# A DLRM tower: ten tables looked up by one-hot matmuls where it was twelve, and the Gram of two samples in one matmul

## The chip, the cores and the metric

The kernel runs on one core of a Trainium2 chip. The time is that of one launch on the device, in microseconds (us), from the first to the last instruction with what the launch itself takes around them. The engines are TensorE (PE in the profile; PEld is its weight load), VectorE (DVE), ScalarE (ACT), GpSimd (POOL) and SyncE (SP, whose queue SPq issues transfers). They run on their own and wait for each other by semaphores.

## The reference

512 samples; each has a dense vector of 128 and one row out of each of 26 tables (one of 125,000 rows, nine of 12,500, eight of 1,250, eight of 1,000; rows of 128). The products of all pairs of its 27 vectors go with the dense vector through three layers.

```python
e = jnp.stack([tbl_0[ids[:, 0]], ..., tbl_25[ids[:, 25]]], axis=1)
combined = jnp.concatenate([dense_features[:, None, :], sparse_features], axis=1)
interactions = jnp.einsum('bnd,bmd->bnm', combined, combined)
interactions_flat = interactions[:, _TRIU_I, _TRIU_J]
z = jnp.concatenate([dense_features, interactions_flat], axis=1)
h = jnp.concatenate([z, r_dense_features], axis=1)
h = jnp.maximum(h @ W_top1 + b_top1, 0.0)
h = jnp.maximum(h @ W_top2 + b_top2, 0.0)
y = h @ W_top3
```

All is float32.

## The kernel before

The samples are taken in four tiles of 128. `vecs_t` (128 x tile x pair of samples x slot x 2) holds, for each sample, its vectors as columns: slot 0 the dense vector, then the tables, and five slots repeated, so that 32 columns of a sample stand side by side. Two ways fill it.

Fourteen tables are **gathered**: GpSimd issues one indirect DMA for each table and tile (`gather`, L316), 56 in all, group by group; a group is up to four slots, a tile four groups, so there are 16 groups. PE transposes a group (`turn`, L401) into one of two PSUM tiles `turned`, and VectorE or ScalarE copies it to `vecs_t` (`copy_slots`, L257; `VECTOR_TURNS` says which are VectorE's). Group n is gathered when `turn` n - 3 is done (`AHEAD` = 2).

Twelve small tables are **looked up** for all 512 samples at once, as products with one-hot matrices. SyncE loads a table whole (`load_table`, L248, three buffers; a load waits until the table three before it is split). ScalarE rounds it to fp32r (`table_hi`, L556), VectorE takes the rest (`table_lo`, L496). A table has 8 or 10 blocks of 125 rows; per block a one-hot matrix of 125 x 512 is made, 6 or 8 of them by VectorE (`make_one_hot`, L488, up to four blocks a comparison) and two by ScalarE (L581, L589). PE multiplies all blocks with `table_hi` (L416), then with `table_lo` (L421), and ScalarE copies the sums to `vecs_t` (L565). The ids that are compared must stand on all partitions: those of table 0 are spread by two matmuls with ones (L450), those of the others by three broadcast DMAs into `ids_all` (L285). The one-hot ring has 16 blocks, the sums have four PSUM buffers.

Then, tile by tile, `products` (L437) computes the Gram of each sample: 128 matmuls of 32 columns by 27, each with its own weights, in turn on four column groups of PE's array, into one of two PSUM buffers `gram`. VectorE and ScalarE copy what is wanted of it to `prods` in 20 copies each (`copy_products`, L268). `layer1` (L350 to L355), `layer2` (L371) and `layer3` (L386) follow; ScalarE applies bias and ReLU, VectorE copies y.

The order on each engine is written by hand: `LOOK_TURNS` (each look-up and the turns behind it), then `TENSOR_STEPS`, `VECTOR_STEPS` and `SCALAR_STEPS`. On PE: the look-ups with turns 0 to 13, products 0, turn 14, products 1, turn 15, products 2 and 3 with layer 1 of tiles 0 and 1 in pieces between them, and the rest of the layers. SyncE issues the weights after table 6.

## Time and profile before

| | |
|---|---|
| median of 3 runs | 135.03 us (133.61 to 135.52) |
| the profiled execution's own time | 133.31 us |
| its span | 131.5 us |
| mean granted clock of TensorE | 0.948 |
| PE busy | 107.2 us (82%), 1534 matmuls |
| PE weight loads | 87.1 us (66%), 1534 |
| VectorE busy | 84.2 us (64%) |
| ScalarE busy | 83.7 us (64%) |
| GpSimd busy | 60.5 us (46%) |
| moved by DMA | 15.87 MB |

A row of a timeline gives the start, the length, the engine and line, the operation with output and inputs, the count, and in brackets how long the engine was idle before and what ended that. A float32 matmul stands in the trace as two passes, each a weight load and a matmul, so the 512 Gram matmuls are 1024 in it; an fp32r matmul or a transpose is one pass. Times of one matmul overlap with the next; the distance from start to start is what a stream of them costs. "issue" is idle time for which the profile shows no releaser. The granted clock is 1.00 at 2.4 GHz and 0.50 at 1.2 GHz.

### The profile page before, as it was taken

The numbers are of one execution on the slowest core, as the hardware profiler recorded it, in microseconds if no ns is written. First come the engines' busy times: TensorE is split into PE (matmuls) and PEld (weight loads), VectorE is DVE, ScalarE is ACT, GpSimd is POOL, SyncE is SP. The second block draws the span as 40 slices with busy tenths as digits, with TensorE's granted clock in tenths as the row PEclk, the third lists the DMA queues.
The fourth block names the chain that finished last, engine by engine and source line by source line (L and its number), as shares of the span: only waits on it lengthen the run. The fifth ranks groups of instructions, "written<-read, shape, count | busy, mean of one in ns | idle before, by whom it ended". The sixth has DMA issues, their size and how long they took to land.

```text
span 131.5 us, 3642 instructions
## 1 busy us (share of the span) xinstructions
PE 107.2 (82%) x1534; PEld 87.1 (66%) x1534; DVE 84.2 (64%) x133; ACT 83.7 (64%) x193; POOL 60.5 (46%) x64
## 2 busy tenths in 40 slices
PE   0139998899993199999989994857799779999993
PEld 0117877555862188888857583656698779997981
DVE  1089999599999457999999900794923923920000
ACT  4389394599999854999977050754813943973112
POOL 2687878878878667788697885000000000000000
PEclk9999999999999869999999999555999999999999
DMA  4999999999999979274111122000000000000000
GB/s 98 220 299 287 363 368 253 253 221 260 388 278 232 212 151 250 60 188 109 45 40 40 40 60 59 11 5 5 5 5 0 7 5 5 0 0 5 0 0 1
DMA packets 4812, 15.87 MB, mean 121 GB/s; under 512 B 1630, under 2 KB 1630, under 8 KB 4540
## 3 DMA queue, kind: packets, MB, share of 16 engines
q1 hardware_dynamic: 2850, 11.45, 32.1%
q0 software_dynamic: 1792, 3.67, 11.7%
q10 hardware_dynamic: 154, 0.51, 1.2%
q8 instruction: 12, 0.20, 0.7%
q14 instruction: 4, 0.03, 0.1%
HBM read 15.63 MB, written 0.00 MB: 119 GB/s over the span
## 4 chain that ended last, share of the span: by engine, by line
PE 52%; POOL 19%; issue 12%; DMA 9%; DVE 5%; ACT 0%; DVEq 0%; ACTq 0%
POOL vecs L316 19%; PE gram L437 10%; PE h_ps L352 10%; PE gram L421 9%; PE gram L416 7%; DMA vecs<-tbl,idx 7%; PE turned L371 5%; PE turned L401 4%; PE h_ps L350 3%; DVE one_hot L488 3%; DMA idx<-idx_rows 2%; DVE table_lo L496 2%; PE gram L386 2%; PE h_ps L355 1%; DVE vecs_t L257 1%
## 5 line engine op out<-in xcount | busy, mean ns | idle before, releaser
L316 POOL DMA_INDIRECT vecs<-tbl,idx x56 | 59.7, 1065 | 20.0 <-issue 15.8
L488 DVE TENSOR_TENSOR one_hot<-ids_all,h_ps 125x2048 fp32r<-125x2048 int32 (+1 forms) x24 | 41.9, 1793 | 1.9 <-PE gram L421 1.9
L416 PE MATMUL gram<-one_hot,table_hi 125*128 125x512 f32 x104 | 31.9, 441 | 3.5 <-DVE one_hot L488 2.2
L268 DVE COPY prods<-gram 32x128 f32<-32x128 f32 (+5 forms) x80 | 19.1, 254 | 20.0 <-PE gram L437 9.2
L416 PEld LDWEIGHTS gram<-one_hot,table_hi 125*128 125x128 f32 x104 | 20.2, 207 | 11.2 <-ACT one_hot L589 3.0
L421 PE MATMUL gram<-one_hot,table_lo 125*128 125x512 f32 x104 | 26.5, 399 | 0.5 <-DVE table_lo L496 0.5
L421 PEld LDWEIGHTS gram<-one_hot,table_lo 125*128 125x128 f32 x104 | 19.9, 193 | 5.7 <-DVE table_lo L496 1.4
L268 ACT COPY prods<-gram 32x128 f32<-32x128 f32 (+5 forms) x80 | 17.4, 235 | 8.5 <-PE gram L437 7.0
L437 PE MATMUL gram<-vecs_t 128*32 128x27 f32 x1024 | 14.3, 208 | 6.7 <-issue 6.5
L437 PEld LDWEIGHTS gram<-vecs_t 128*32 128x32 f32 x1024 | 12.3, 126 | 9.2 <-issue 8.5
L496 DVE TENSOR_TENSOR table_lo<-table,table_hi 125x1024 fp32r<-125x1024 f32 (+1 forms) x12 | 15.7, 1308 | 1.9 <-ACT table_hi L556 1.9
L589 ACT ACTIVATE one_hot<-distance,one 125x512 fp32r<-125x512 f32 x24 | 15.9, 711 | 1.6 <-PE gram L421 1.5
L565 ACT COPY vecs_t<-gram 128x512 f32<-128x512 f32 (+1 forms) x12 | 9.7, 807 | 10.6 <-PE gram L421 10.6
L352 PE MATMUL h_ps<-prods,w_sb 128*128 128x128 f32 x112 | 15.9, 279 | 0.0
L556 ACT CAST table_hi<-table 125x1024 fp32r<-125x1024 f32 (+1 forms) x12 | 13.4, 1115 | 3.5 <-DMA table<-tbl 3.5
L581 ACT ACTIVATE distance<-ids_all,row_of 125x512 f32<-125x512 int32 x22 | 14.7, 716 | 0.0
L401 PE MATMUL turned<-ident,vecs 128*128 128x128 f32 x56 | 10.1, 306 | 5.3 <-DMA vecs<-tbl,idx 5.2
L352 PEld LDWEIGHTS h_ps<-prods,w_sb 128*128 128x128 f32 x112 | 13.9, 192 | 0.1
L539 ACT ACTIVATE h<-h_ps,small_sb 128x128 f32<-128x128 f32 x16 | 4.9, 368 | 12.8 <-PE h_ps L355 12.8
L401 PEld LDWEIGHTS turned<-ident,vecs 128*128 128x128 f32 x56 | 7.3, 155 | 7.6 <-DMA vecs<-tbl,idx 6.4
L471 DVE COPY distance<-gram 1x128 f32<-1x128 f32 x4 | 1.1, 279 | 13.0 <-PE gram L386 13.0
L371 PE MATMUL turned<-h,w_sb 128*128 128x128 f32 x64 | 8.1, 280 | 0.0
(33 smaller groups left out, 54.3 us busy)
## 6 DMA issues: line engine op xcount, KB each, us to landing
table<-tbl SPq DMA_DIRECT2D x7, 448.0 KB
table<-tbl SPq DMA_DIRECT2D x4, 560.0 KB
ids_all<-ids_look SPq DMA_DIRECT2D x1, 2048.0 KB, 16.1
w_sb<-w SPq DMA_DIRECT2D x1, 1536.0 KB, 9.5
vecs<-tbl,idx POOLq DMA_INDIRECT x56, 7.0
ids_all<-ids_look SPq DMA_DIRECT2D x1, 512.0 KB, 9.3
w_sb<-w SPq DMA_DIRECT2D x1, 512.0 KB, 10.0
table<-tbl ACTq DMA_DIRECT2D x1, 448.0 KB
```

The source lines that it names most:

```text
L268: return copy(dst.rearrange("p c (h b) -> p c h b", h=HALVES), src.rearrange("p h c b -> p c h b"))
L316: nc.gpsimd.indirect_dma_start(out=vecs[:, t % KEEP, s - 1, :], out_offset=None, in_=tables[f], in_offset=bass.IndirectOffsetOnAxis(ap=idx ...
L352: nc.tensor.matmul(to, w1_sb[:, 1 + c, cols], prods[:, t % 2, c - 1, :], start=False, stop=(c == CHUNKS))
L371: mm = nc.tensor.matmul(h2_ps[o], w2_sb[:, c, o * P:(o + 1) * P], h1[:, t % 2, c, :], start=(c == 0), stop=(c == H1 // P - 1))
L401: mm = nc.tensor.transpose(turned[n % 2][:, i, :], vecs[:, t % KEEP, s - 1, :] if s else dense_rows[:, t, :], ident[:])
L416: nc.tensor.matmul(looked_up[j % SUMS], table_hi[0:TP, j % PARTS, c, :], one_hot[0:TP, k % HOT, :], start=(c == 0), stop=False)
L421: nc.tensor.matmul(looked_up[j % SUMS], table_lo[0:TP, j % PARTS, c, :], one_hot[0:TP, k % HOT, :], start=False, stop=(c == NBLK[j] - 1)). ...
L437: mm = nc.tensor.matmul(gram_cols[t % 2][QUAD * q:QUAD * q + ROWS, blk // HALF, :, blk % HALF], x[:, 0:ROWS], x[:, 0:N], start=True, stop= ...
L488: nc.vector.tensor_tensor(one_hot[0:TP, k % HOT:k % HOT + n, :], ids.to_broadcast([TP, n, B]), rows.to_broadcast([TP, n, B]), ALU.is_equal ...
L496: nc.vector.tensor_tensor(table_lo[0:TP, j % PARTS, 0:NBLK[j], :], table[0:TP, j % RAW, 0:NBLK[j], :], table_hi[0:TP, j % PARTS, 0:NBLK[j] ...
L581: nc.scalar.activation(distance[0:TP, i, :], ids, ACT.Square, bias=at, scale=-1.0).then_inc(distance_ok, 1)
L589: nc.scalar.activation(one_hot[0:TP, k % HOT, :], distance[0:TP, i, :], ACT.Relu, bias=one[0:TP], scale=-1.0).then_inc(hot_act, 1)
```

## The change

- Ten tables are looked up and sixteen gathered (64 gathers). The gathered slots are 1 to 9 and 15 to 21, so a group is always four gathered slots; the third of each tile (slots 9, 15, 16, 17) is copied in two pieces. The slots repeated are now 10 to 14. The dense vectors of all tiles are transposed in one step after look-up 0 and copied by ScalarE.
- The ids of the ten tables are loaded as ten rows. Those of each table are spread by PE, two matmuls of 512 columns with `pick` (ten selector matrices), into four PSUM banks in turn. The broadcast loads are gone.
- `products` takes two samples of one parity in a matmul: 64 columns of weights, 54 moving columns, 64 matmuls a tile, on two column groups. Of the four 32 x 27 blocks of one such product two are used. It fills four PSUM banks, the same for each tile, so it waits for the copies of the tile before. The sums have two buffers in place of four.
- The last look-up is made in two halves of 256 samples. Tile 0's product stands between them. Turns 8 to 15 and layer 1 stand between the later products. VectorE copies turns 1, 3, 5 and all from 7 on.
- The weights are issued after the last table. `AHEAD` is 3.

```diff
-LOOKED_UP = 12
+LOOKED_UP = 10
-SUMS = 4
+SUMS = 2
-AHEAD = 2
-IDS_PARTS = [(1, 2), (2, 4), (4, LOOKED_UP)]
-WEIGHTS_AFTER = 6
+AHEAD = 3
+WEIGHTS_AFTER = LAST
-TURN_AFTER = [0, 1, 2, 3, 4, 5, 5, 6, 7, 8, 9, 10, 11, 11]
+TURN_AFTER = [1, 2, 3, 4, 5, 6, 7, 8]
...
-        gram = [psum(f"gram{i}", [P, HALVES, 512]) for i in range(2)]
+        bank = psum("bank", [P, 2 * BANKS, 512])
+        gram_cols = bank[:, BANKS:, 0:2 * N * RUN].rearrange("p k (m b) -> p k m b", b=RUN)
+        looked_up = [bank[:, j % SUMS, :] for j in range(LAST)]
+        looked_up_half = [bank[:, (LAST + h) % SUMS, 0:B // 2] for h in range(2)]
+        ids_for_dve = [bank[:, BANKS + i, :] for i in range(2)]
+        ids_for_act = [bank[:, BANKS + 2 + i, :] for i in range(2)]
...
+            def spread_ids(j):
+                if j == 0:
+                    pe.wait_ge(pick_ok, 1)
+                    pe.wait_ge(row_f_ok, 1)
+                if j >= 2:
+                    pe.wait_ge(hot_dve, sum(BY_VECTOR[:j - 1]))
+                    pe.wait_ge(distance_ok, BY_SCALAR * (j - 1))
+                for ids in (ids_for_dve[j % 2], ids_for_act[j % 2]):
+                    nc.tensor.matmul(ids, pick[:, j, :], ids_rows_f[:], start=True, stop=True).then_inc(ids_ps_ok, 1)
...
             def look_up(j):
...
+                if j + 2 < LOOKED_UP:
+                    spread_ids(j + 2)
                 pe.wait_ge(lo_ok, j + 1)
...
-            def products(t, layer1_of=None):
+            def products(t):
                 tile_is_out(pe, t)
-                if t == 0:
-                    pe.wait_ge(look_out, LOOKED_UP)
-                if t >= 2:
-                    pe.wait_ge(prods_dve, BY_ENGINE * (t - 1))
-                    pe.wait_ge(prods_act, BY_ENGINE * (t - 1))
-                for blk in range(BLOCKS):
-                    for q in range(QUADS):
-                        r = QUAD * q + blk
-                        x = vecs_t[:, t, r // 2, :, r % 2]
-                        mm = nc.tensor.matmul(
-                            gram_cols[t % 2][QUAD * q:QUAD * q + ROWS, blk // HALF, :, blk % HALF],
-                            x[:, 0:ROWS], x[:, 0:N], start=True, stop=True)
+                pe.wait_ge(look_out, LOOKED_UP + t // 2)
+                if t >= 1:
+                    pe.wait_ge(prods_dve, BY_ENGINE * t)
+                    pe.wait_ge(prods_act, BY_ENGINE * t)
+                for b in range(BLOCKS):
+                    for g in range(P // WIDE):
+                        first = BLOCKS * g + b // 2 * 2
+                        both = vecs_t[:, t, first:first + 2, :, b % 2]
+                        mm = nc.tensor.matmul(gram_cols[WIDE * g:WIDE * (g + 1), b // RUN, :, b % RUN],
+                                              both.rearrange("p x s -> p (x s)"), both[:, :, 0:N],
+                                              start=True, stop=True)
```

On PE, from the end of the look-ups on (L401 a turn, L437 the Gram, L350 and L352 layer 1), before:

```order
L401 MATMUL turned<-ident,vecs 128x128 x7
L437 MATMUL gram<-vecs_t 32x27 x128
L401 MATMUL turned<-ident,vecs 128x128 x4
L437 MATMUL gram<-vecs_t 32x27 x128
L401 MATMUL turned<-ident,vecs 128x128 x3
L437 MATMUL gram<-vecs_t 32x27 x43
L350 MATMUL h_ps<-dense_t,w_sb 128x128
L352 MATMUL h_ps<-prods,w_sb 128x128 x4
L350 MATMUL h_ps<-dense_t,w_sb 128x128
```

The same place of the change (L436 a turn, L484 and L490 a half of the last look-up, L506 the Gram, L371 and L373 layer 1; all PSUM is `bank`):

```order
L436 MATMUL bank<-ident,vecs 128x128 x4
L484 MATMUL bank<-one_hot,table_hi 128x256 x10
L490 MATMUL bank<-one_hot,table_lo 128x256 x10
L436 MATMUL bank<-ident,vecs 128x128 x4
L506 MATMUL bank<-vecs_t 64x54 x64
L484 MATMUL bank<-one_hot,table_hi 128x256 x10
L490 MATMUL bank<-one_hot,table_lo 128x256 x10
L436 MATMUL bank<-ident,vecs 128x128 x8
L506 MATMUL bank<-vecs_t 64x54 x64
L436 MATMUL bank<-ident,vecs 128x128 x4
L371 MATMUL bank<-dense_t,w_sb 128x128
L373 MATMUL bank<-prods,w_sb 128x128 x4
```

The last look-up is in two pieces with product 0 between them, each product has 64 matmuls, and turns and a whole layer 1 stand between products where pieces of layer 1 stood within them.

On VectorE, between the copies of products 0 and 1 (L268 the copies, L257 slots), before:

```order
L268 COPY prods<-gram 21x2x32
L268 COPY prods<-gram 10x2x32
L268 COPY prods<-gram 10x4x32
L257 COPY vecs_t<-turned 128x4x64x2
L268 COPY prods<-gram 32x4x32 x2
L268 COPY prods<-gram 32x2x32 x2
```

The same place of the change (L295 the copies, L282 slots, L579 the sum of the two dense weights):

```order
L295 COPY prods<-bank 10x2x32
L295 COPY prods<-bank 10x4x32
L282 COPY vecs_t<-bank 128x64x2
L282 COPY vecs_t<-bank 128x3x64x2
L282 COPY vecs_t<-bank 128x4x64x2
L579 TENSOR_TENSOR w_sb<-w_sb 128x512
L295 COPY prods<-bank 32x4x32 x2
```

Where one turn's slots stood (turn 14), there are now turns 10 (in two pieces) and 11 and the weight sum.

On SyncE's queue, around the weights (L299 to L301), before:

```order
L248 DMA table<-tbl 13x1024
L299 DMA w_sb<-w 128x3072
L300 DMA w_sb<-w 128x1024
L301 DMA small_sb<-small 128x8
L248 DMA table<-tbl 112x1024
```

The same of the change (L274 the tables, L318 to L320 the weights):

```order
L274 DMA table<-tbl 112x1280
L274 DMA table<-tbl 13x1280
L318 DMA w_sb<-w 128x3072
L319 DMA w_sb<-w 128x1024
L320 DMA small_sb<-small 128x8
L322 DMA y<-distance 1x512
```

The weights have moved behind all tables.

## Rows read from the trace of the kernel before

**Rows 1.** The first line of the page.

```profile
span 131.5 us, 3642 instructions
```

**Rows 2.** The chain of waits: start us, us, what.

```profile
36.50 8.89 DMA vecs<-tbl,idx
...
53.24 1.82 PE gram L421 x8
...
55.06 0.44 PE turned L401 x4
...
57.79 2.27 PE gram L421 x10
...
110.44 1.79 PE turned L371 x16
```

**Rows 3.** Timeline of PE: start us, us, engine, line, operation, count, idle before.

```profile
45.44 1.12 PE L401 MATMUL turned<-ident,vecs 128*128 128x128 f32 x4 [4.89 <-DMA vecs<-tbl,idx]
```

**Rows 4.** Timeline of ScalarE (ACT), same columns, the cast of table 3.

```profile
24.45 1.05 ACT L556 CAST table_hi<-table 125x1024 fp32r<-125x1024 f32 x1 [3.15 <-DMA table<-tbl]
```

**Rows 5.** Timeline of VectorE (DVE): comparisons, and a copy out of a turn.

```profile
7.12 3.42 DVE L488 TENSOR_TENSOR one_hot<-h_ps,row_of 125x2048 fp32r<-125x2048 f32 x2 [5.74 <-PE h_ps L450]
...
11.59 3.41 DVE L488 TENSOR_TENSOR one_hot<-ids_all,h_ps 125x2048 fp32r<-125x2048 int32 x2
...
46.59 0.69 DVE L257 COPY vecs_t<-turned 128x512 f32<-128x512 f32 x1 [2.24 <-PE turned L401]
...
50.29 4.48 DVE L488 TENSOR_TENSOR one_hot<-ids_all,h_ps 125x2048 fp32r<-125x2048 int32 x2 [1.87 <-PE gram L421]
...
56.09 4.55 DVE L488 TENSOR_TENSOR one_hot<-ids_all,h_ps 125x2048 fp32r<-125x2048 int32 x3
```

**Rows 6.** Timeline of PE, Gram matmuls.

```profile
77.72 2.77 PE L437 MATMUL gram<-vecs_t 128*32 128x27 f32 x203
...
82.05 0.76 PE L437 MATMUL gram<-vecs_t 128*32 128x27 f32 x53 [1.55 <-issue]
...
85.72 1.93 PE L437 MATMUL gram<-vecs_t 128*32 128x27 f32 x128 [0.75 <-issue]
...
89.44 1.05 PE L437 MATMUL gram<-vecs_t 128*32 128x27 f32 x58 [1.80 <-issue]
...
97.94 0.93 PE L437 MATMUL gram<-vecs_t 128*32 128x27 f32 x84
...
108.43 0.25 PE L437 MATMUL gram<-vecs_t 128*32 128x27 f32 x3 [0.67 <-issue]
```

**Rows 7.** Windows: stretch, length, busy time (count) by engine, granted clock, DMA.

```profile
82.50:92.60 10.10, 7.32 (x351) 6.22 (x341) 7.36 (x29) 6.26 (x29) 0.00 (x0) 0.50 0.02 5
...
92.80:110.30 17.50, 15.45 (x528) 14.22 (x528) 8.04 (x33) 8.47 (x37) 0.00 (x0) 1.00 0.02 5
```

**Rows 8.** The page: the instruction queue (packets, MB, share), and the gathers' group.

```profile
q8 instruction: 12, 0.20, 0.7%
...
L316 POOL DMA_INDIRECT vecs<-tbl,idx x56 | 59.7, 1065 | 20.0 <-issue 15.8
```

**Rows 9.** DMA issues, all and from 60 to 85 us: count, KB, us to landing.

```profile
ids_all<-ids_look SPq DMA_DIRECT2D x1, 2048.0 KB, 16.1
...
vecs<-tbl,idx POOLq DMA_INDIRECT x15, 2.7
```

**Rows 10.** Timeline of GpSimd (POOL), three of the 56 gathers.

```profile
3.90 1.10 POOL L316 DMA_INDIRECT vecs<-tbl,idx  x1 [2.22 <-DMA idx<-idx_rows]
...
15.29 1.66 POOL L316 DMA_INDIRECT vecs<-tbl,idx  x1 [0.30 <-issue]
...
80.42 0.94 POOL L316 DMA_INDIRECT vecs<-tbl,idx  x1 [0.30 <-issue]
```

**Rows 11.** Timeline of VectorE, the copy of products 0.

```profile
82.85 5.26 DVE L268 COPY prods<-gram 32x128 f32<-32x128 f32 x20 [7.48 <-PE gram L437]
```

**Rows 12.** Timeline of PE, the last matmuls.

```profile
128.95 0.67 PE L386 MATMUL gram<-h,small_sb 128*1 128x128 f32 x4 [0.16 <-ACT h L548]
```

More of the change, by code:

```diff
@@ L47 @@
 GATHERED = by_size[LOOKED_UP:]
-SLOT_TABLE = [None] + GATHERED + LOOKUPS
-TURNED = 1 + len(GATHERED)
+LAST = LOOKED_UP - 1
+GATHERED_SLOTS = list(range(1, FIRST_R)) + list(range(FIRST_V, FIRST_V + len(GATHERED) - FIRST_R + 1))
+LOOKED_UP_SLOTS = [n for n in range(1, N) if n not in GATHERED_SLOTS]
+SLOT_TABLE = [None] * N
+for n, f in list(zip(GATHERED_SLOTS, GATHERED)) + list(zip(LOOKED_UP_SLOTS, LOOKUPS)):
+    SLOT_TABLE[n] = f
 NBLK = [TABLE_ROWS[f] // TP for f in LOOKUPS]
@@ L192, in dlrm_tower @@
         lo_ok = sem("lo_ok")
-        rows_ps_ok = sem("rows_ps_ok")
         one_ok = sem("one_ok")
@@ L222, in looked, with pieces @@
             return FIRST_HOT[j] + NBLK[j]
+        def pieces(n):
+            return len(runs(GROUPS[n % NG]))
         def outs(by_vector, n):
-            return sum(2 if i % NG == 0 else 1 for i in range(n + 1) if (i in VECTOR_TURNS) == by_vector)
+            return sum(pieces(i) for i in range(n + 1) if (i in VECTOR_TURNS) == by_vector)
         def turn_is_out(engine, n):
@@ L362, in mlp2 @@
             def mlp2(t):
+                last = {0: 13, 1: 15}.get(t)
+                if last is not None:
+                    turn_is_out(pe, last - 1)
+                    turn_is_out(pe, last)
                 if t >= 1:
@@ L387, in mlp3, with turn_dense @@
                                           start=(c == 0), stop=(c == H2 // P - 1))
                 mm.then_inc(y_ok, 1)
+            def turn_dense():
+                pe.wait_ge(ident_ok, 1)
+                pe.wait_ge(dense_in, 16)
+                for t in range(TILES):
+                    mm = nc.tensor.transpose(turned[1][:, t, :], dense_rows[:, t, :], ident[:])
+                mm.then_inc(dense_ok, 1)
             def turn(n):
                 t, g = TURNS[n]
-                slots = GROUPS[g]
@@ new lines, in look_up_half @@
+            def look_up_half(h):
+                j = LAST
+                samples = slice(B // 2 * h, B // 2 * (h + 1))
+                pe.wait_ge(look_out, LAST - 1 + h)
+                if h == 0:
+                    pe.wait_ge(hi_ok, j + 1)
+                for c in range(NBLK[j]):
+                    k = FIRST_HOT[j] + c
+                    if h == 0 and c < BY_VECTOR[j]:
+                        pe.wait_ge(hot_dve, sum(BY_VECTOR[:j]) + c + 1)
+                    elif h == 0:
+                        pe.wait_ge(hot_act, BY_SCALAR * j + c - BY_VECTOR[j] + 1)
+                    nc.tensor.matmul(looked_up_half[h], table_hi[0:TP, j % PARTS, c, :],
+                                     one_hot[0:TP, k % HOT, samples], start=(c == 0), stop=False)
+                if h == 0:
+                    pe.wait_ge(lo_ok, j + 1)
+                for c in range(NBLK[j]):
+                    k = FIRST_HOT[j] + c
+                    mm = nc.tensor.matmul(looked_up_half[h], table_lo[0:TP, j % PARTS, c, :],
+                                          one_hot[0:TP, k % HOT, samples], start=False, stop=(c == NBLK[j] - 1))
+                mm.then_inc(half_ok, 1)
@@ L445, in products @@
                 mm.then_inc(gram_ok, 1)
-            pe.wait_ge(ones_ok, 1)
-            pe.wait_ge(row_f_ok, 1)
-            for ids in (ids_for_dve, ids_for_act):
-                nc.tensor.matmul(ids, ones[:], ids_row_f[:], start=True, stop=True).then_inc(ids_ps_ok, 1)
+            spread_ids(0)
+            spread_ids(1)
             for step, i in TENSOR_STEPS:
@@ L453, in _ @@
                     turn(i)
+                elif step == "dense":
+                    turn_dense()
                 elif step == "look":
                     look_up(i)
+                elif step == "look half":
+                    look_up_half(i)
                 elif step == "products":
                     products(i)
-                elif step == "products and layer1":
-                    products(i, i - 2)
                 elif step == "layer1":
@@ L512, in _ @@
                 split_table(j)
-            for n, after in enumerate(TURN_AFTER):
-                if after >= LOOKED_UP - 2 and n in VECTOR_TURNS:
-                    copy_slots(dve, nc.vector.tensor_copy, slots_dve, n)
             for step, i in VECTOR_STEPS:
```

211 lines of the change are left out of this document (107 added, 104 removed).

## The prediction

> **What bounds it now.** I read the page first, then the chain of waits, then each engine's timeline, and last windows of the Gram lines. One profiled execution has a span of 131.5 us [rows 1] and its own time is 133.31 us, so 1.8 us lie outside the span; all sums below are spans of that execution. Its time is 1.3% under the median of 135.03 us.
>
> The span falls into four stretches. (a) Up to about 45 us GpSimd's gathers and the DMA lead: the chain has one gather that takes 8.89 us to land [rows 2], PE stands 4.89 us for it [rows 3], and before that ScalarE stood 3.15 us for table 3 [rows 4]. (b) Up to 77.7 us the look-ups run at VectorE's pace: comparing and splitting one table takes it 4.47 us with 8 blocks (starts 7.12 and 11.59) and 5.80 us with 10 (50.29 and 56.09) [rows 5], while PE needs 2 x 1.82 plus 0.44 us for 8 blocks and a turn, and 2 x 2.27 plus 0.44 for 10 [rows 2]. (c) Up to 108.7 us come the Gram matmuls. In the trace one Gram matmul is two passes of a 32-wide load and 27 columns. 84 passes without a gap take 0.93 us, so (0.93 - 0.19) / 83 = 8.9 ns each, and a tile's 256 would take 2.3 us. They take over 5 (tile 0: 77.72 to 82.81), because PE stands for "issue": [0.75] before 85.72, [1.80] before 89.44, with 128 passes (256 instructions) between them, hence 3.72 us for 256 instructions [rows 6]. From 82.5 to 92.6 us the granted clock is 0.50, the lower level, and PE busy only 7.3 of 10.1 us; after 92.8 it is 1.00 [rows 7]. (d) The rest is MLP work, PE nearly without a gap.
>
> The page names the queue "instruction" with 12 transfers and 0.20 MB [rows 8], which fits refills of about 256 instructions. The Trainium skill (Runtime: NRT & Kernel Launch, Instruction fetch mechanics) says just this: instructions come in blocks of 256. It calls the fetch mostly hidden; the trace disagrees here, with 3.72 us a block in the open.
>
> **The change, part by part.** *Look-ups.* Two 10-block tables go from the look-ups to the gathers. VectorE starts as before, at 7.12 us [rows 5], since the id spread waits for the same kind of small load and cast; `pick` is one copy ahead of that, in idle time. Eight tables x 4.47, two of 5.80, and the slot copies of turns 1, 3, 5 at about 0.6 each [rows 5]: 7.12 + 35.8 + 11.6 + 1.8 = 56.3 us. Reading ids from PSUM costs nothing by the first comparison, which does it already in 3.42 us against 3.41 [rows 5]. The spreads add 2 x 0.227 us to PE per table: 3.64 + 0.44 + 0.45 = 4.5 us, just level with VectorE's 4.47. I cost them at nothing; without this cover they would cost 0.5 x 8 = 4 us. The broadcast id loads disappear (the last moves 2,048 KB and takes 16.1 us to land [rows 9]), and the weights queue behind table 9, whose wait (split of table 6) ends near 39 us; 2 MB then have until 76 us. So the waits of 3.15 and 4.89 us go. After the split at 56.3 PE does 10 half-width matmuls (0.116 each by half of 0.227), turn 8, and starts product 0 at 58.3, 19.4 us earlier than 77.7.
>
> *Gathers.* 64 instead of 56. The trace has a gather at 3.90 and the last at 80.42 [rows 10]; spacing is 1.25 us (0.94 plus 0.31), more where VectorE's split overlaps: the gather at 15.29 takes 1.66. Over 56 gathers the excess is 59.7 - 56 x 0.94 = 7 us [rows 8] for 12 splits. With 10 splits: 3.9 + 63 x 1.25 + 5.8 + 0.9 = 89.4, and I allow 90.3. Landing takes 2.7 us from the issue once the queues are empty [rows 9], so turn 15 may start at 92.1. `turned` waits do not bind: gather group n wants turn n - 4, which is over 5 us older.
>
> *Gram.* 64 matmuls a tile, 128 passes, each with a 64-wide load and 54 columns, two column groups at once in place of four. No row shows it. Below: if only the instructions cost, 128 x 8.9 ns = 1.1 us. Between: a 32-wide group holds its place for 4 x 8.9 = 35.6 ns [rows 6], a full 128 x 128 pass for 1.79 / 16 = 112 ns [rows 2]; on the straight line 64 wide is 61 ns, two at once 30.5, times 128 = **3.9 us**. Above: no overlap, 7.8 us. I take 3.9, as the two rows enclose it. It is more than the bare 2.3 us, since half of each product is of two different samples and thrown away; but a product is now one block of 256 instructions, so the 3.72 us of a fetch hide behind it. The Trainium skill (TensorEngine Tiling (Array Packing), Theoretical Speedup) speaks against the change: up to 4x for 32-wide tiles, 2x for 64-wide. By it two groups of double length need twice the bare time, an estimate of 4.6 us, and the sum would grow by 2.8.
>
> At the lower clock 128 passes took 1.93 us [rows 6], (1.93 - 0.2) / 127 = 13.6 ns, 1.5 times 8.9. Product 1 comes after some 4 us in which PE waits, and before 45.4 and at 82 us idle or broken work was followed by the lower clock. I give product 1 the lower clock: 6.0 instead of 3.9, +2.1.
>
> *One Gram buffer.* Product t now waits until both engines have copied product t - 1; before, it had another buffer. A copy is 5.26 us on VectorE [rows 11]. What stands behind the waiting product on PE is a turn and a whole layer 1; VectorE waits for the turn, ScalarE for layer 1. The walk, at full clock, with 0.2 us from a PE end to a reader: product 0 58.3 to 62.2; half look-up, 20 x 0.116, to 64.6; turn 9 to 65.0; slots 9 to 65.8; copy 0 to **71.1**; product 1 to 75.0; turn 11, its slots and the weight sum (0.6 each) to 76.9; copy 1 to 82.1; product 2 to **86.1**; copy 2 to 91.5 (layer 1 of tile 1 beside it); slots 13 to 92.1; layer 2 of tile 0, 16 passes, 1.8, to 94.0; turns 14, 15 to 94.9; their slots to 96.0; product 3 to **100.0**. So four products with what lies between take 41.7 us, where they took 31.0: +10.7, and +12.8 with the clock. Each extra us of a product counts four times.
>
> *Tail.* After product 3 PE has layer 1 of tile 2 (40 passes x 0.112 = 4.5, behind it copy 3 ends at 105.4), layer 2 of tile 1 (1.8), layer 1 of tile 3 (4.5), two layer 3 (1.1), two layer 2 (3.6), 0.5 waiting for ScalarE, two layer 3 (1.1): 100.0 + 17.1 = 117.0. From the last matmul's start at 128.95 to the end of the span are 2.5 us [rows 12]; with half of those in the 1.1 above, 119.0. The tail is 19.0 us after 22.8: -3.8, for layer 1 of tile 2 now runs beneath copy 3.
>
> Sum: 131.5 - 19.4 + 12.8 - 3.8 = **121.1 us**. Outside the span 1.8: 122.9; on the scale of the median, x 135.03 / 133.31, 124.5. I say 124.
>
> **The rivals.**
> 1. *The gathers become the bound.* If a product takes 2.3 us or less, PE reaches turn 15 before its gather lands: product 3 at about 93, end 114 (116 in time). For it: the last gather is only 2.4 us ahead of the walk. Against: the 112 ns of a wide pass.
> 2. *The lower clock holds through all products.* 6.0 four times is 119.0 + 8.4 = 127.4, and some layer passes at 0.5 bring 128 to 131. For it: 0.50 from 82.5 to 92.6 with PE busy 73%. Against: 1.00 from 92.8 with layers between the Gram parts, as in the new order.
> 3. *PE becomes the bound of the look-ups* (a wait for the spreads in place of that for the ids): +4, 125.
> 4. *The other side: the two 64-wide groups don't overlap.* Place: each of the four products. Price: 7.8 - 3.9 = 3.9 four times, 134.6 us, slower by 2.4%. It decides from 7.0 us a product (no change), 55 ns a pass; from 7.7 it is slower by 2%. Against: four 32-wide groups clearly overlap, 8.9 ns beside 112.
> 5. *The change doesn't do what it says*: the look-ups stay held by some DMA (weights in front of gathers of groups 7 and 8) and lose 5 us of the 19.4; 126.
>
> **Numbers.** Forecast with products of 3.4 to 4.6 us and one or two of them at the lower clock, span 117 to 125: 0.55. Rival 1: 0.13. Rival 2: 0.14. Rivals 3 and 5: 0.10. Products between 6.4 and 7.7, no change: 0.04; rival 4: 0.04 or less. A measurement of this kernel can tell about 2% from no change, that is 132.3 and 137.7 us. The range, 117.5 to 132, leaves out half of rival 1 and the no-change and slower cases. Faster 0.92, same 0.05, slower 0.03.
>
> **What would show it.** VectorE's last split ends near 56 and the first Gram pass stands near 58; 128 passes of a product in 3.9 us, with next to no "issue"; VectorE's copies start near 66, 77, 86, 100; the last gather issues near 89 and turn 15 doesn't wait for it; granted clock 0.5 about product 1; PE without gaps in the last 17 us. The prediction is wrong first in the pass time, four times on the path, then in the clock, and then if PE's waits for copies carry turns late enough to hold gathers back.

## The result, and the profile after

The changed kernel takes 127.34 us (median of 4 runs, 125.99 to 128.6), the kernel before 135.28 us beside it (133.61 to 136.31): a ratio of 0.953, with an interval of 0.946 to 0.961. The ratios in this document compare only the fast runs of each kernel (within 1.5% of its fastest), so they are not the quotients of the medians beside them (here 0.941). It is faster by 4.7%, where the forecast of 124 against 135 said 8%. The profiled execution took 128.6 us, the longest of the four; its span is 126.8, where the sum said 121.1, and the spans of the other three are 124.2 to 125.7.

The page of the changed kernel: span, busy time of PE, the granted clock in 40 slices, the instruction queue, and the groups of the gathers and of the Gram matmuls.

```profile
span 126.8 us, 2619 instructions
...
PE 107.2 (85%) x1028; PEld 90.0 (71%) x1028; DVE 77.5 (61%) x132; ACT 72.8 (57%) x176; POOL 67.6 (53%) x72
...
PEclk9999999999999999999999965799999999999999
...
q8 instruction: 8, 0.13, 0.5%
...
L334 POOL DMA_INDIRECT vecs<-tbl,idx x64 | 66.7, 1042 | 21.4 <-issue 18.6
...
L506 PE MATMUL bank<-vecs_t 128*64 128x54 f32 x512 | 18.4, 239 | 6.8 <-DVE prods L295 5.7
```

The answer to [rows 8]: 8 transfers of instructions in place of 12. PE's 107.2 us are what they were; the span around them is 4.7 us shorter.

The chain of waits of the changed kernel (start us, us, what): look-up 0, look-up 2 with the start of the next, and the slots that stand ahead of the copy of product 0.

```profile
9.64 3.75 PE bank L461 x8
13.40 1.15 PE bank L448 x2
14.54 3.71 PE bank L468 x8
18.26 0.85 PE bank L420 x4
...
24.20 1.85 PE bank L461 x8
26.05 0.66 PE bank L448 x2
26.71 2.05 PE bank L468 x8
28.76 0.44 PE bank L436 x4
29.20 1.83 PE bank L461 x8
...
69.44 0.69 DVE vecs_t L282
```

Beside [rows 2] two things are new. The chain runs through PE from 9.64 us to product 0 at 62.32, with 0.12 us of "issue" as its only gap: no DMA stands in it, so the stalls of [rows 3] and [rows 4] are gone, and so is VectorE's pace. A table takes PE 29.20 - 24.20 = 5.00 us: 1.85 for `table_hi`, 0.66 for the two spreads (L448), 2.05 for `table_lo`, 0.44 for the turn. And look-up 0 takes 9.5 us, from 9.64 to 19.1: its passes take 3.75 / 8 = 0.47 us, twice 1.85 / 8 = 0.23. That is the lower of the two clock levels. (The record of the clock begins with its first change, here at 19.16 us. Before that the windows and the row `PEclk` print full clock, so pass times have to tell it.)

PE's timeline of the changed kernel: the four products and the end (start, length, line, operation, count, idle before).

```profile
62.32 4.06 PE L506 MATMUL bank<-vecs_t 128*64 128x54 f32 x128
...
75.55 6.25 PE L506 MATMUL bank<-vecs_t 128*64 128x54 f32 x128 [5.71 <-DVE prods L295]
...
89.13 4.06 PE L506 MATMUL bank<-vecs_t 128*64 128x54 f32 x128
...
103.50 4.06 PE L506 MATMUL bank<-vecs_t 128*64 128x54 f32 x128 [1.00 <-DVE vecs_t L282]
...
123.86 1.03 PE L412 MATMUL bank<-h,small_sb 128*1 128x128 f32 x8
```

Where [rows 6] had broken pieces with "issue" between them, each product is one piece. The granted clock around product 1 (stretch, length, busy time of PE, PEld, DVE, ACT and POOL, clock, DMA):

```profile
69.90:73.70 3.80, 0.00 (x0) 0.00 (x0) 3.45 (x16) 3.48 (x18) 2.83 (x3) 1.00 0.20 52
73.80:75.50 1.70, 0.00 (x0) 0.00 (x0) 1.54 (x7) 0.28 (x2) 1.35 (x2) 0.50 0.16 41
75.50:80.50 5.00, 4.95 (x93) 4.98 (x95) 0.58 (x2) 0.00 (x0) 3.78 (x5) 0.50 0.22 55
```

It falls while PE stands idle, and most of product 1 runs at the lower level. VectorE's timeline around product 0 shows why product 1 waits 5.71 us.

```profile
62.24 0.69 DVE L282 COPY vecs_t<-bank 128x512 f32<-128x512 f32 x1 [1.40 <-PE bank L436]
69.44 0.69 DVE L282 COPY vecs_t<-bank 128x512 f32<-128x512 f32 x1 [6.50 <-PE bank L436]
70.05 5.25 DVE L295 COPY prods<-bank 32x128 f32<-32x128 f32 x20
```

Product 0 ends at 66.4. VectorE stands idle 6.50 us until 69.44, since `VECTOR_STEPS` puts slots 9 ahead of products 0, and turn 9 stands on PE behind the second half of look-up 9. Only then does it copy the products, and product 1 waits for that copy, as there is one Gram buffer. ScalarE does likewise: it moves the second half's sums at 69.00 us and copies product 0 from 69.40.

In sums: product 0 starts at 62.3 in place of 77.7 (-15.4); from there to the end of the last product it takes 45.2 us in place of 31.0 (+14.2); the tail takes 19.2 in place of 22.8 (-3.6). 131.5 - 15.4 + 14.2 - 3.6 = 126.7.

### The profile page after: what moved, and what is told of

The parts are those of the page before. It is cut to its first block, busy times and chain, and to the rows that moved or that the text cites. A ratio compares the mean times of both kernels' runs of the same rounds, so it can differ in the third digit from the quotient of the medians.

```text
span 126.8 us, 2619 instructions
## 1 busy us (share of the span) xinstructions
PE 107.2 (85%) x1028; PEld 90.0 (71%) x1028; DVE 77.5 (61%) x132; ACT 72.8 (57%) x176; POOL 67.6 (53%) x72
## 3 DMA queue, kind: packets, MB, share of 16 engines
q0 software_dynamic: 2048, 4.20, 12.8%
## 4 chain that ended last, share of the span: by engine, by line
PE 79%; DVE 13%; DMA 3%; issue 2%; ACT 1%; SPq 0%; DVEq 0%; ACTq 0%
PE bank L468 16%; PE bank L461 15%; PE bank L506 15%; DVE prods L295 8%; PE bank L373 7%; PE bank L397 6%; PE bank L448 5%; PE bank L436 5%; DMA ids_rows<-ids_look 3%; DVE vecs_t L282 3%; PE bank L371 2%; PE bank L490 2%; PE bank L484 2%; DVE one_hot L549 2%; PE bank L412 2%
## 5 line engine op out<-in xcount | busy, mean ns | idle before, releaser
L549 DVE TENSOR_TENSOR one_hot<-bank,row_of 125x2048 fp32r<-125x2048 f32 (+1 forms) x21 | 36.4, 1777 | 7.9 <-PE bank L448 4.9
L295 ACT COPY prods<-bank 32x128 f32<-32x128 f32 (+5 forms) x80 | 17.4, 235 | 19.0 <-PE bank L506 17.5
L295 DVE COPY prods<-bank 32x128 f32<-32x128 f32 (+5 forms) x80 | 19.1, 254 | 9.4 <-PE bank L506 7.5
L506 PE MATMUL bank<-vecs_t 128*64 128x54 f32 x512 | 18.4, 239 | 6.8 <-DVE prods L295 5.7
L506 PEld LDWEIGHTS bank<-vecs_t 128*64 128x64 f32 x512 | 18.0, 154 | 7.7 <-issue 6.5
L461 PE MATMUL bank<-one_hot,table_hi 125*128 125x512 f32 x74 | 21.1, 431 | 1.3 <-DVE one_hot L549 1.3
L468 PE MATMUL bank<-one_hot,table_lo 125*128 125x512 f32 x74 | 21.0, 430 | 0.0
L282 DVE COPY vecs_t<-bank 128x512 f32<-128x512 f32 (+2 forms) x14 | 8.3, 611 | 17.5 <-PE bank L436 17.4
L468 PEld LDWEIGHTS bank<-one_hot,table_lo 125*128 125x128 f32 x74 | 14.3, 203 | 6.0 <-issue 2.9
L461 PEld LDWEIGHTS bank<-one_hot,table_hi 125*128 125x128 f32 x74 | 14.5, 207 | 4.7 <-issue 2.0
L373 PE MATMUL bank<-prods,w_sb 128*128 128x128 f32 x112 | 15.1, 275 | 0.0
L373 PEld LDWEIGHTS bank<-prods,w_sb 128*128 128x128 f32 x112 | 13.8, 192 | 0.0
L448 PE MATMUL bank<-ids_rows_f,pick 10*128 10x512 f32 x20 | 8.4, 513 | 6.3 <-ACT ids_rows_f L664 6.3
L448 PEld LDWEIGHTS bank<-ids_rows_f,pick 10*128 10x128 f32 x20 | 3.7, 222 | 9.6 <-issue 9.4
L436 PE MATMUL bank<-ident,vecs 128*128 128x128 f32 x64 | 9.4, 275 | 0.1
```

What stands on the lines that cost most here:

```text
L295: return copy(dst.rearrange("p c (k b) -> p c k b", k=BANKS), src.rearrange("p k c b -> p c k b"))
L373: nc.tensor.matmul(to, w1_sb[:, 1 + c, cols], prods[:, t % 2, c - 1, :], start=False, stop=(c == CHUNKS))
L436: mm = nc.tensor.transpose(turned[n % 2][:, i, :], vecs[:, t % KEEP, g, i, :], ident[:])
L448: nc.tensor.matmul(ids, pick[:, j, :], ids_rows_f[:], start=True, stop=True).then_inc(ids_ps_ok, 1)
L461: nc.tensor.matmul(looked_up[j], table_hi[0:TP, j % PARTS, c, :], one_hot[0:TP, k % HOT, :], start=(c == 0), stop=False)
L468: nc.tensor.matmul(looked_up[j], table_lo[0:TP, j % PARTS, c, :], one_hot[0:TP, k % HOT, :], start=False, stop=(c == NBLK[j] - 1)).then_in ...
```

## The experiments

Three things were to be told apart: why the look-ups end 4 us late, whether the wide Gram matmul is worth what it throws away, and what of product 1's wait and clock can be had back. Besides, two parts of the change were undone, one of them on top of another edit. The kernels ran in three groups, each beside the kernel before on the same chip.

**The groups differ.** In the second group the kernel before took 134.42 us. In the first and third it took 141.72 and 141.26 us; these two are called disturbed below. In the first of them the changed kernel is not faster:

> The changed kernel once more, as the measure for the runs beside it. Its first execution had a span of 126.8 us, products of 4.06 us at full clock, one of 6.25 us, and 4.97 us a table in the look-ups. Both theories: the same within 1%. Where TensorE's clock first rises may lie elsewhere (19.2 us in the first trace, 14.2 us in that of before).

Measured: 149.11 us (148.11 to 150.47), ratio 1.075, interval 1.041 to 1.109. This is the changed kernel, unedited. All eight kernels of the two disturbed groups show the same in their traces. PE's timeline of `e8_warm_start` (below), a piece of product 0, and product 2:

```profile
67.42 1.71 PE L509 MATMUL bank<-vecs_t 128*64 128x54 f32 x43 [0.30 <-ACT vecs_t L632]
69.45 0.37 PE L509 MATMUL bank<-vecs_t 128*64 128x54 f32 x5 [0.33 <-issue]
70.18 0.28 PE L509 MATMUL bank<-vecs_t 128*64 128x54 f32 x2 [0.36 <-issue]
...
107.38 4.06 PE L509 MATMUL bank<-vecs_t 128*64 128x54 f32 x128
```

PE's passes come in bursts of 1 to 6, 0.71 us or a multiple apart. The last burst of this stretch starts between 78.0 and 79.3 us in all eight traces (the two narrow kernels have one more pause at 83), that of another between 96 and 100.3, and products 2 and 3 are whole again. All eight have products 0 and 1 in these stretches, so the traces don't tell whether the time or the work draws the bursts; pieces of the look-ups are broken too. It is a disturbance from outside the kernel: the same kernel, unedited, ran without it in the second group. GpSimd, VectorE and ScalarE have waits in all eight that end on "remote", that is on something outside this core's record (GpSimd up to 2.79 us at a time); the six traces of the other runs have none. What it is no trace shows. It is not bound to one chip by the numbers on record: those are chip 12 for the first group and chip 1 for the second and the third. That it costs the changed kernel more (149 against 127) than the one before (142 against 135) would fit that its products 0 and 1 lie in those stretches, while the kernel before has look-ups with long passes up to 77 us; that is argued only, as no trace of the kernel before was taken in these groups. From the disturbed groups only pieces outside the bursts are used below.

**The same again in the undisturbed group.**

> The changed kernel again, as the measure beside the three that follow. On the chip of the runs before, every kernel stood still at the same times after the start (24 to 28, 67 to 79, 90 to 97 us), the changed one as the others, and it took 149 us. If that is a matter of that chip, this run takes 126 to 129 us; if it is a matter of the kernel, it comes back.

Measured: 127.83 us (126.93 to 128.21), ratio 0.959, interval 0.949 to 0.969. Product 0 starts at 62.13, product 1 takes 6.02 us. It is the reference for the rest of the second group.

**The spread over 128 rows.** `pick` and `ids_rows_f` get 128 partitions, zeros below the ids; the same sums.

```diff
-        ids_rows_f = sb("ids_rows_f", [LOOKED_UP, B], F32R)
-        pick = sb("pick", [LOOKED_UP, LOOKED_UP, P], F32R)
+        ids_rows_f = sb("ids_rows_f", [P, B], F32R)
+        pick = sb("pick", [P, LOOKED_UP, P], F32R)
...
```

> The id spread contracts over all 128 partitions (zeros below the ten ids) in place of ten; same columns, same number of matmuls. Theory A (each table pays for two changes between an operand of 10 rows and one of 125, and TensorE is the bound of the look-ups): the spreads take 0.45 us a table in place of 0.66, the pass over table_lo 1.82 in place of 2.04, a table 4.5 to 4.6 us in place of 4.97, product 0 starts 3 to 3.5 us earlier (near 59) and the span shrinks by about 3 us, 2.5%. Theory B (the columns alone cost, or VectorE and ScalarE set the pace): no piece changes, and the time stays within 0.5%.

Measured: 148.97 us, ratio 1.073, interval 1.057 to 1.088, disturbed. The pieces before 34 us are whole. Its chain of waits:

```profile
20.55 1.84 PE bank L462 x8
22.39 0.47 PE bank L449 x2
22.86 1.83 PE bank L469 x8
24.69 0.44 PE bank L437 x4
25.13 1.85 PE bank L462 x8
```

A table takes 25.13 - 20.55 = 4.58 us in place of 5.00. The spreads fall from 0.66 to 0.47 and the pass behind them from 2.05 to 1.83, though they multiply 128 rows in place of 10. So it is the step from 125 rows to 10 and back that costs 0.2 us each time, and not the work; the step from 125 to 128 shows no such cost. The Trainium skill (TensorEngine Tiling (Array Packing), Key Properties) says that a change of tiling mode drains TensorE, without a price. The trace fits this if a matmul over 10 rows is in another mode, which no run here shows by itself; the price would then be these 0.2 us. What the edit is worth in the time this run doesn't tell.

**One sample a matmul.**

```diff
-                        both = vecs_t[:, t, first:first + 2, :, b % 2]
-                        mm = nc.tensor.matmul(gram_cols[WIDE * g:WIDE * (g + 1), b // RUN, :, b % RUN],
-                                              both.rearrange("p x s -> p (x s)"), both[:, :, 0:N],
-                                              start=True, stop=True)
+                        for x in range(2):
+                            at = WIDE * g + QUAD * x
+                            v = vecs_t[:, t, first + x, :, b % 2]
+                            mm = nc.tensor.matmul(gram_cols[at:at + ROWS, b // RUN, x * N:(x + 1) * N, b % RUN],
+                                                  v[:, 0:ROWS], v[:, 0:N], start=True, stop=True)
```

> The Gram by one sample a matmul again (32 columns of weights, 27 moving, 128 matmuls a tile on four column groups), written where the wide one wrote; all else as in the change. Theory A (instruction refill bounds the narrow form): 512 instructions a product at 3.72 us for 256, so products of 5 to 7 us with gaps named issue, where the array alone needs 2.3 us; the span grows by 4 to 10 us over the change. Theory B (the array is the bound and the narrow form wastes nothing): products of 2.3 us, four times 1.7 us less on the path, the span 5 to 7 us shorter.

Measured: 156.64 us, ratio 1.131, interval 1.117 to 1.144, that is 7.5 us above `again`, both disturbed. Repeated on top of the wide spread and the early copy (`e6_pad_copy` below):

> This is e6_pad_copy with the Gram of one sample a matmul (256 passes of 32 rows by 27 columns a product) in place of two (128 passes of 64 by 54), the values and all else alike. It repeats e2_narrow without the disturbance that stood over that comparison. Theory A (a product of 256 instructions waits open for its instructions: 1.51 + 2.38 + 1.25 us were seen in e2_narrow's product 2): every product takes 4.9 to 5.4 us from its first pass to its last instead of 4.06, with one idle stretch of about 2.4 us inside whose releaser is issue, and the median is 2.5 to 5 us above e6_pad_copy's 119.69, so 122.2 to 124.7. Theory B (the stretch was the disturbance of that chip, and the passes themselves cost 2.3 to 2.8 us a product): each product is 1.3 to 1.8 us shorter, three of them stand on the path, and the median is 114.3 to 116.

Measured: 156.25 us (155.57 to 156.99), ratio 1.110, interval 1.101 to 1.119, disturbed once more and 9.4 us above `e8_warm_start` of its group. Bursts of a few passes may cost a form with twice the passes more, so these medians don't say what the form costs undisturbed. Products 2 and 3 lie outside the bursts. PE's timeline of `e9_narrow`:

```profile
111.99 1.51 PE L509 MATMUL bank<-vecs_t 128*32 128x27 f32 x154
...
115.39 1.07 PE L509 MATMUL bank<-vecs_t 128*32 128x27 f32 x102 [1.89 <-issue]
...
126.78 0.92 PE L509 MATMUL bank<-vecs_t 128*32 128x27 f32 x82 [1.00 <-DVE vecs_t L283]
...
128.69 1.78 PE L509 MATMUL bank<-vecs_t 128*32 128x27 f32 x128 [0.98 <-issue]
...
132.42 0.85 PE L509 MATMUL bank<-vecs_t 128*32 128x27 f32 x46 [1.95 <-issue]
```

The passes alone are cheap: 1.51 / 154 = 9.8 ns, 2.5 us for 256. But a refill stands open once or twice a product: product 2 takes 4.47 us from first pass to last, product 3 6.49 us (part of it at the lower clock). The wide form takes 4.06 in every product at the higher clock outside the bursts, with nothing open. In `e2_narrow` the same two take 5.15 and 4.95 us, each with one stretch of "issue" of 2.4 us. So A's mechanism is there, with products on both sides of its 4.9 to 5.4: the wide matmul, whose passes are 1.6 us dearer, still gains 0.4 to 1.1 us in three of the four and 2.4 in the one that ran partly at the lower clock. The 128 passes from 128.69 on, 256 instructions, take 3.73 us with what stands open, as 3.72 in [rows 6]; the wide form spends 4.06 on as many. What that is worth in the time of an undisturbed run was not measured.

**The copy of products 0 ahead of turn 9's slots.** On VectorE one entry of the table moves (shown); on ScalarE the move of the second half's sums goes behind its products 0.

```diff
-    ("turn", 7), ("turn", 8), ("turn", 9), ("products", 0), ("turn", 10), ("turn", 11), ("weights", 0),
+    ("turn", 7), ("turn", 8), ("products", 0), ("turn", 9), ("turn", 10), ("turn", 11), ("weights", 0),
...
```

> VectorE copies product 0 before the slots of turn 9, and ScalarE before it moves the second half of the last look-up; nothing else is moved. Theory A (the copies of product 0 stood 3.5 us behind turn 9 and the second half, and this lies on the path): the copies start at 66.5 in place of 70.05, product 1 starts at 72 in place of 75.5, and since TensorE then waits 2 us in place of 5.7 the clock may stay up and product 1 take 4.06 in place of 6.25: the span is 3.5 to 5.7 us shorter. Theory B (the gathers are as late): product 2 or 3 then waits for a gather, and the span shrinks by less than 2 us.

Measured in the first, disturbed group: 147.07 us, ratio 1.057, interval 1.026 to 1.088; it doesn't tell. In the second:

> The copies of product 0 first, as before on the other chip, where the copies of product 0 began as soon as it was done. Theory A: against the changed kernel beside it 3.5 us less, 5.7 if product 1 keeps the full clock. Theory B: under 2 us.

Measured: 119.53 us, ratio 0.897, interval 0.887 to 0.907. PE's timeline, products 0 and 1:

```profile
62.20 4.07 PE L506 MATMUL bank<-vecs_t 128*64 128x54 f32 x128
...
71.81 4.06 PE L506 MATMUL bank<-vecs_t 128*64 128x54 f32 x128 [2.09 <-DVE prods L295]
```

VectorE's, the copy of products 0:

```profile
66.31 5.25 DVE L295 COPY prods<-bank 32x128 f32<-32x128 f32 x20 [3.49 <-issue]
```

The copy starts at 66.31, as product 0 ends, and PE's wait falls from 5.7 to 2.09 us. With so short a wait the lower clock doesn't come: product 1 takes 4.06 us. In `again2`, which ran beside it and has product 0 at the same place (62.13), product 2 starts at 88.71; here it starts at 83.20, 5.5 us earlier. 3.6 of that is the wait and 2.0 the clock. The two spans differ by 5.5 us too (120.9 and 126.4). So theory A holds. The median moved by more, 8.3 us: the five times are 119.3, 119.3, 119.5, 122.6 and 122.7, and the profiled one is the highest. The other 3 us of the lower three times are as much as an early first rise of the clock is worth in the next kernel; that this is their cause is argued only, as no trace was taken of them.

**Filler on PE in the wait ahead of product 1.** 24 matmuls of 512 columns on old operands, whose sums nobody reads.

```diff
+                    if t == 1:
+                        for i in range(24):
+                            nc.tensor.matmul(bank[:, LAST % SUMS, :], table_lo[0:TP, LAST % PARTS, 0, :],
+                                             one_hot[0:TP, FIRST_HOT[LAST] % HOT, :], start=True, stop=True)
                     pe.wait_ge(prods_dve, BY_ENGINE * t)
```

> 24 matmuls of 512 columns, whose sums nobody reads, fill TensorE's wait of 5.7 us before product 1. Theory A (product 1 takes 6.25 us for the granted clock of 0.50 alone, which the wait brought on): granted clock 1.00 there, product 1 in 4.06 us, span 2 us shorter than the change. Theory B (product 1 is slow for another reason: copies beside it, a refill of instructions): it stays near 6.2 us and the span is the same or, by the matmuls put in, up to 0.3 us longer.

Measured: 123.02 us (122.89 to 123.87), ratio 0.927, interval 0.918 to 0.937. PE's timeline, look-up 0, product 0, the filler and product 1:

```profile
9.28 3.52 PE L461 MATMUL bank<-one_hot,table_hi 125*128 125x512 f32 x8 [1.30 <-DVE one_hot L553]
...
13.39 2.12 PE L468 MATMUL bank<-one_hot,table_lo 125*128 125x512 f32 x8
...
59.02 4.06 PE L510 MATMUL bank<-vecs_t 128*64 128x54 f32 x128
...
66.29 5.71 PE L502 MATMUL bank<-one_hot,table_lo 125*128 125x512 f32 x24
72.04 4.06 PE L510 MATMUL bank<-vecs_t 128*64 128x54 f32 x128
```

Kept busy, product 1 takes 4.06 us in place of 6.02: the clock's share is 2.0 us. The other 3 us are not the filler's. They came before it: the clock rose at 12.4 us, look-up 0 had `table_lo` at the higher level (2.12 in place of 3.78), and product 0 starts at 59.02 in place of 62.13. All kernels of this group but `e6_pad_copy` begin with the same program up to here, and by the record of the clock the rise stood at 12.40, 18.44, 19.04 and, in the first result, 19.16 us. Where product 0 starts follows it: 59.02 for a rise at 12.40, 62.13 for 18.44, 62.20 for 19.04, 62.32 for 19.16. From the end of look-up 0 to product 0 the chains of all four take 43.1 to 43.2 us, with PE busy throughout, so the difference lies in look-up 0 and its start: 6.7 us from 9.28 on here, 9.5 us from 9.64 on in the first result.

**Wide spread and early copy together.**

> Spreads over 128 partitions and the copies of product 0 first, both. In the first trace of the spreads over 128 partitions a table took 4.59 us and not 4.97, the spreads 0.46 and the pass behind them 1.84. Theory A: product 0 starts at 59 in place of 62.3; its copies 3.5 us earlier again; the span 120 us in place of 126.8, or 118 if the clock stays up for product 1. Theory B (gathers become the bound: the last is issued at 88.8 and lands at 92): turn 15 stands at 92 and later than TensorE is free, and the span is 121 to 122.

Measured: 119.69 us (119.18 to 120.02), ratio 0.901, interval 0.894 to 0.908. The span is 117.4 us. VectorE's last split and the slots behind it:

```profile
55.20 1.48 DVE L558 TENSOR_TENSOR table_lo<-table,table_hi 125x1280 fp32r<-125x1280 f32 x1
56.59 0.68 DVE L283 COPY vecs_t<-bank 128x512 f32<-128x512 f32 x1
```

PE's last `table_lo` pieces ahead of product 0, and products 0 and 1:

```profile
56.73 1.45 PE L491 MATMUL bank<-one_hot,table_lo 125*128 125x256 f32 x10 [0.66 <-DVE table_lo L558]
...
58.74 4.06 PE L507 MATMUL bank<-vecs_t 128*64 128x54 f32 x128
...
68.35 4.06 PE L507 MATMUL bank<-vecs_t 128*64 128x54 f32 x128 [2.09 <-DVE prods L296]
```

Here the clock rose at 15.61 us, look-up 0 took 7.6 us, 3.0 more than a full-clock one, and yet product 0 starts at 58.74: with 4.58 us a table PE catches up, and VectorE bounds the look-ups again, as PE's wait of 0.66 us for the last split shows. Theory A held; PE reaches turn 15 at 92 us without a wait for a gather. The medians of this kernel and `e3_copy_first2` (119.69 and 119.53) are the same; what the wide spread brings is that its four times lie within 0.8 us, where the other's spread over 3.4.

**Filler on PE at the start.** On top of the last kernel: 9 matmuls over a zeroed tile ahead of the first spread, 2 behind it.

```diff
+            pe.wait_ge(idle_ok, 1)
+            idle_passes(9)
             spread_ids(0)
             spread_ids(1)
+            idle_passes(2)
...
```

> This is e6_pad_copy with filler work on TensorE at the very start: 9 matmuls of 512 columns over a zeroed tile ahead of the first spread of ids and 2 more ahead of look-up 0. In the profile of e6_pad_copy the granted clock stood at 0.50 until 15.61 us, and look-up 0, which starts at about 9.6 us, ran the first 6 us of its work at half pace: 3 us lost. Theory A (the clock rises on work that TensorE has done, so filler from about 1.5 us brings the rise forward): the rise comes at or before 10 us in the trace, look-up 0 takes about 4.6 us instead of 7 to 9, product 0 starts at 55.5 to 57 instead of 58.74, the median is 116.5 to 118 instead of 119.69. Theory B (the rise does not follow TensorE's work, it comes when it comes, between 11.8 and 19.0 us as in the traces so far): product 0 at 58 to 62, median 119 to 122. A third outcome: the rise comes early but VectorE's 4.47 us a table has no slack at the start, and the median stays within 1 us of 119.69.

Measured: 146.9 us, ratio 1.043, interval 1.035 to 1.051, disturbed. PE's timeline of the first 14 us is whole:

```profile
1.46 3.79 PE L516 MATMUL bank<-idle 128*128 128x512 f32 x9 [1.46 <-DVE idle L571]
5.09 1.08 PE L451 MATMUL bank<-ids_rows_f,pick 128*128 128x512 f32 x4
...
8.96 2.88 PE L464 MATMUL bank<-one_hot,table_hi 125*128 125x512 f32 x8 [2.33 <-ACT table_hi L624]
...
12.15 2.00 PE L471 MATMUL bank<-one_hot,table_lo 125*128 125x512 f32 x8
```

The filler ran at the lower level (0.42 us a pass), the spreads right behind it at the higher (0.27): the record has the rise at 4.63 us, earlier than in any other trace. The matmuls of look-up 0 took 5.0 us (8.96 to 13.98) in place of 6.4 in `e1_pad` (8.98 to 15.36), whose rise stood at 13.70. So theory A holds for the clock, by one trace. What it is worth in the time stays open, since the run is disturbed and VectorE may bound the look-ups anyway.

**The ids by DMA again** (on top of `e3_copy_first`): two broadcast transfers for tables 2 to 9, no spreads in `look_up`, row numbers in PSUM.

```diff
+            load_ids(0)
             load_table(sp, 2)
+            load_ids(1)
...
-                if j + 2 < LOOKED_UP:
-                    spread_ids(j + 2)
...
```

> This is e3_copy_first with one part of the change undone: the ids of tables 2 to 9 come to every partition by two broadcast transfers (0.5 and 1.5 MB) instead of being spread by TensorE, and VectorE compares them with row numbers that lie in PSUM, as in the kernel before. Only the ids of tables 0 and 1 are still spread. Theory A (the transfers were what held the tables back): the first tables come late, ScalarE waits 2 to 6 us in all for a table between 15 and 45 us, product 0 starts at 62 to 66 although TensorE has 0.9 us less to do a table, and the median is 121 to 126 against 119.53 of e3_copy_first2. Theory B (with ten tables and the weights behind the last, the queues have room): the waits for tables stay under 0.5 us, the pace falls from 4.98 to about 4.5 us a table (VectorE's work), product 0 starts at 58 to 59.5 and the median is 116 to 117.5.

Measured: 147.99 us, ratio 1.054, interval 1.043 to 1.065, against 1.057 (1.026 to 1.088) for `e3_copy_first` in the other disturbed group: no difference that can be told there. In its trace no wait for a table stands in the look-ups, which speaks against theory A; but PE's broken stretches gave the transfers more time than they would have, so theory B isn't shown either.

**The weights issued behind table 6.**

```diff
-WEIGHTS_AFTER = LAST
+WEIGHTS_AFTER = 6
```

> This is the changed kernel with one part undone: the weights (2.1 MB) are issued behind table 6 again and not behind table 9. Theory A (they would hold up tables 7 to 9 and the gathers): ScalarE waits 2 to 4 us for table 7 or 8, product 0 starts at 64 to 66 instead of 62.1 to 62.3, median 129.5 to 132 against 127.83 and 127.34. Theory B (the tables are asked for about three look-ups ahead, some 15 us, and a transfer of 2.1 MB fits beside them): no new wait for a table, median 127 to 128.5; the wait of 1.58 us for the sum of two weights before layer 1 of tile 0 is gone, but what stands on the path behind it gains at most that.

Measured: 147.72 us, ratio 1.051, interval 1.040 to 1.062, against 1.075 (1.041 to 1.109) for `again`, both disturbed and in different groups. ScalarE's casts of tables 7, 8 and 9 start at 47.85, 52.17 and 56.28 us, with other work of ScalarE in between and no wait for DMA. This speaks for theory B: where the weights stand makes no difference that these runs can tell. But here too PE's broken stretches gave the transfers more time, so it isn't shown.

## Why the prediction was right, and where it was off

The direction, the range and the mechanism held; the gain was 3.4 points smaller than forecast. How the 15.4 us up to product 0 divide between the two tables that are no longer looked up (11.6 us of VectorE's work by the sum) and the DMA stalls that are gone (3.15 and 4.89) no run tells, as the two that undid loads alone were disturbed. In spans of the profiled executions, the 5.7 us between 126.8 and 121.1 are 4.0 up to product 0, and 1.7 spread over what follows. One row of the kernel before is needed here, from PE's timeline, `table_hi` of its look-up 0:

```profile
9.55 3.75 PE L416 MATMUL gram<-one_hot,table_hi 125*128 125x512 f32 x8 [2.15 <-DVE one_hot L488]
```

- *Look-ups, "I cost them at nothing".* This is the step that failed, by 4.0 us (62.3 for 58.3), together with the next. The spread was sized at 2 x 0.227 = 0.45 us; it cost 0.66, and 0.2 more in the pass behind it, so PE's table took 5.0 us and not 4.5, and VectorE waited for PE (1.45 us before its comparison at 22.97, about 0.4 at others); its last split ended at 60.2, where 56 was given as a sign. That is rival 3, and its condition, cover gone, came true; that its price of 4 comes out to the tenth is luck, since it was 0.5 x 8 for the spreads and nothing for the clock.
- *Look-ups, the clock, which the sum left out.* The pace alone would not have cost 4: from 9.6 us, nine tables at 5.0 and the first half of the last with its turn (59.10 to 62.32, 3.2) end at 57.8, no later than VectorE's 58.3; `e4_warm`, whose look-up 0 lost only 1.7 us to the clock, had 59.02. Look-up 0 runs at the lower clock, here the whole of it, 4.5 us more than 5.0. In the kernel before, look-up 0 was slow too (the row above), and PE caught up, since it stood waiting for VectorE and for DMA later on. The change took those waits away. `e6_pad_copy` gives PE slack again; its last split ends at 56.7 us and product 0 starts at 58.74, where the prediction had 56.3 and 58.3. That the late clock decides is shown by the pass times of look-up 0 and by the 43.1 to 43.2 us that follow it in all four traces, with one early rise against three late ones; nobody set the rise in an undisturbed run. That the pace matters is shown by the one kernel with the wide spread.
- *Pass time 3.9 us a product.* Measured 4.06, 31.7 ns a pass for 30.5. Four times 0.16 makes 0.6 of the 1.7 us. Rival 4 (no overlap, 7.8) and rival 1 (2.3 or less) fell. The Trainium skill (TensorEngine Tiling (Array Packing), Theoretical Speedup) led to an estimate of 4.6; the trace gives 4.06, nearer to the straight line between the two rows.
- *No open refills.* Right: no "issue" within the four products. In the two narrow kernels they came back, 0.98 to 2.38 us apiece outside the bursts. One reading was wrong: 3.72 us is the distance from block to block (85.72 to 89.44), of which 1.93 were passes and 1.80 stood open, so not 3.72 but 1.80 were "in the open". The conclusion doesn't hang on it, as 3.9 us of passes are longer than 3.72 either way; the margin is small.
- *The clock of product 1, 6.0 us.* Right, 6.25 and 6.02 in two traces, and its cause, the idle PE ahead of it, is shown by `e4_warm` and `e3_copy_first2`. Rival 2 fell: the other products ran at 1.00.
- *One Gram buffer.* The walk had VectorE wait for turn 9 before copying products 0, and the time it gave was right: product 1 began 13.2 us behind product 0 where the walk had 12.8. But it was taken as given. It is an entry in a table of steps, and moving it, with ScalarE's order to match, took 5.5 us from the span: 3.6 us of waiting and 2.0 of clock. Of the two single edits that ran undisturbed, this and the filler, it gave more.
- *Gathers.* Predicted last issue at 89.4, measured 88.82. Rival 5 fell, and the DMA stalls are gone. The term for the weights was not needed.
- *Tail.* Predicted 19.0, measured 19.2.

## What to carry to other kernels

When an edit moves work onto an engine that was just level with the one that set the pace, cost it with what it does to its neighbours (a matmul over 10 rows slowed the next one, over 125, too) and ask what delay at the start that engine used to catch up with; an engine without slack carries it to the end. After a buffer is made single, look for what stands ahead of its release in the order of the engine that empties it: here one step moved on each of two engines took 5.5 us from the span, more than the 4.7 us that the whole change gave. And a ratio from one occasion need not hold on another: the same two kernels gave 0.953 and 0.959 on two occasions and 1.075 on a third.

## What the runs showed of the hardware

- Two matmuls over 10 rows between matmuls over 125 cost 0.2 us more than two over 128 rows, and the pass behind them another 0.2 (0.66 + 2.05 against 0.47 + 1.83 us).
- The clock's first rise came between 11.82 and 19.16 us in 13 traces with PE's first work near 6 us, at 11.82 in `e3_copy_first` and at 19.04 in `e3_copy_first2`, the same kernel; with filler from 1.46 us it came at 4.63. Whether chance, the chip or something in the program decides it was not settled: the times of `e4_warm` all lie near 123 and those of `again2` near 128.
- PE can stand for "issue" for 1 to 2.4 us where 32-wide passes of 9.8 ns use up 256 instructions, with 3.7 us from block to block; it doesn't where the same count takes 4.06 us. That these are refills of its instructions is inferred from the count.
- In two of three groups PE's passes came in bursts 0.71 us or a multiple apart, in stretches that ended within 1.2 and 4.2 us of each other in eight kernels; the changed kernel took 149 us there and the one before 142.
